# Row maxima of attention scores read two PSUM banks at a time, with thirteen of the first group's units inside the first stage's last step

## The reference

```python
x = L0_attn_query                                      # 8 x 1024 x 256, float32
x = x + 0.5 * _L0_ffn_ref(_layernorm(x), ...)          # two matrices, top-2 gate over 7 logits
x = x + _L0_attn_ref(_layernorm(x), ...)               # 16 heads of 16 columns, causal
x = x + 0.5 * _L0_ffn_ref(_layernorm(x), ...)

# _L0_attn_ref, b = 8, t = 1024, D = 16
q = q / math.sqrt(D)
scores = jnp.einsum('bhqd,bhkd->bhqk', q, k)
scores = jnp.where(causal[None, None], scores, -inf)
attn = jax.nn.softmax(scores, axis=-1)
out = jnp.einsum('bhqk,bhkd->bhqd', attn, v)
```

## Time and profile before

| | us |
|---|---|
| median of 3 runs | 1353.83 (1350.99 to 1354.71) |
| the profiled execution | 1353.6 |
| its span, first to last instruction | 1351.8 |
| PE, DVE, ACT, POOL busy | 1245.0, 1138.3, 920.7, 435.0 |
| mean granted clock of PE | 0.963 |

### The profile page before, as it was taken

How to read it: one execution, slowest core, us unless ns; L and a number is a source line. 1 busy time by engine, 2 the same in 40 slices (tenths; PEclk the granted TensorE clock), 3 DMA queues, 4 the chain that set the end, 5 groups by cost and what they waited for, 6 DMA issues and landing times. The chain is left out here.

```text
span 1351.8 us, 37753 instructions
## 1 busy us (share of the span) xinstructions
PE 1245.0 (92%) x9324; PEld 825.8 (61%) x9324; DVE 1138.3 (84%) x4510; ACT 920.7 (68%) x1858; POOL 435.0 (32%) x843
## 2 busy tenths in 40 slices
PE   4999999978999999999999999999999997699996
PEld 3988888964554454554554554554554543599996
DVE  4788888749999999999999999999999994367775
ACT  3666666630777777777777777777777777356654
POOL 3333333301222222222222222222322322467772
PEclk9999999985899999999999999999999999699998
DMA  3366666881564564664664664664664663556651
GB/s 113 141 225 225 225 225 225 220 274 37 78 107 81 99 106 80 101 104 80 103 102 80 103 102 80 104 101 80 106 99 80 106 99 107 158 180 196 192 165 63
DMA packets 121900, 174.12 MB, mean 129 GB/s; under 512 B 44012, under 2 KB 71788, under 8 KB 121804
## 3 DMA queue, kind: packets, MB, share of 16 engines
q1 hardware_dynamic: 121816, 173.30, 56.4%
HBM read 96.08 MB, written 76.02 MB: 127 GB/s over the span
## 5 line engine op out<-in xcount | busy, mean ns | idle before, releaser
L1000 ACT ACTIVATE b_probs<-bank 128x512 f32<-128x512 f32 x1152 | 597.4, 612 | 135.4 <-PE bank L1124 131.6
L1027 DVE CUSTOM_DVE_ANT_0 b_junk<-bank,mask 128x512 bf16<-128x512 f32 (+3 forms) x1032 | 446.8, 488 | 1.4 <-issue 1.2
L1030 DVE TENSOR_REDUCE b_pm<-bank 128x1 f32<-128x512 f32 x516 | 322.4, 683 | 19.7 <-PE bank L1101 18.7
L1143 PE MATMUL bank<-b_probs,b_vx 128*32 128x512 f32 (+3 forms) x3072 | 310.3, 499 | 4.2 <-ACT b_o L985 1.9
L1124 PE MATMUL bank<-qs,ks 50*128 50x512 f32 (+3 forms) x1056 | 293.6, 383 | 4.3 <-ACT b_probs L1000 0.4
L1101 PE MATMUL bank<-ks,qs 48*128 48x512 f32 (+3 forms) x1056 | 277.2, 390 | 10.9 <-PEq L443 6.3
L1101 PEld LDWEIGHTS bank<-ks,qs 48*128 48x128 f32 x1056 | 165.1, 193 | 134.6 <-DVE b_pm L1030 61.5
L145 POOL TENSOR_TENSOR hold_pool<-zero 128x1 f32<-128x1 f32 x192 | 37.4, 195 | 629.9 <-ACT b_probs L1000 474.3
L1124 PEld LDWEIGHTS bank<-qs,ks 50*128 50x128 f32 x1056 | 159.7, 188 | 57.3 <-ACT b_probs L1000 52.4
L960 POOL TENSOR_SCALAR_AFFINE_SELECT b_probs<-b_probs 128x512 f32<-128x512 f32 x256 | 158.5, 638 | 0.0
L1143 PEld LDWEIGHTS bank<-b_probs,b_vx 128*32 128x32 f32 x3072 | 71.1, 109 | 109.6 <-issue 80.9
(11 more groups left out here) (120 smaller groups left out, 1993.8 us busy)
## 6 DMA issues: line engine op xcount, KB each, us to landing
scr_qk<-a_qk SPq DMA_DIRECT2D x64, 512.0 KB, 3.2
qs<-scr_qk SPq DMA_DIRECT2D x132, 128.0 KB, 4.5
ks<-scr_qk SPq DMA_DIRECT2D x132, 128.0 KB, 5.1
scr_o<-b_o SPq DMA_DIRECT2D x64, 256.0 KB, 3.7
b_qs<-scr_qk SPq DMA_DIRECT2D x66, 128.0 KB, 4.0
b_ks<-scr_qk SPq DMA_DIRECT2D x66, 128.0 KB, 4.6
a_x<-x SPq DMA_DIRECT2D x16, 512.0 KB, 3.5
scr_x<-a_x SPq DMA_DIRECT2D x16, 512.0 KB, 2.7
```

Of the source, the lines that this page charges most:

```text
L1000: act.activation(probs[:, PROB_BUF[s], h, :], score_bank(g, t, last)[:], ACT.Exp).then_inc(p_ready, 1)
L1027: ins = dve.tensor_tensor_reduce(junk[:, t % MB, off:off + w], src, mask[:, BANK - w:BANK], 1.0, 0.0, ALU.add, ALU.max, pm[:, g.buf, 0, pl ...
L1030: ins = dve.tensor_reduce(pm[:, g.buf, 1, place(h), i:i + 1], src, AX.X, ALU.max)
L1143: last = pe.matmul(o_bank[2 * D * h:2 * D * (h + 1), col:col + w], vx[g.buf][:, j, h, :], probs[:, PROB_BUF[src], h, off:off + w], start=( ...
```

## The change

A maximum unit is now two banks wide: 1024 columns, filled by PE in two tiles and read by DVE with one instruction for each block of 128 queries in it, across the border of the banks (`dve_unit`). All are of the masked kind. A group has 18 units in place of 36 tiles; the plain maxima and the joining of halves fall away, and `part` has two steps. A unit's two tiles are of the same half of the partitions. The four banks are now two pairs, and PE fills a pair when DVE has read all of it. PE's order in a slot becomes maximum, score, three times, then the values, maximum, score, and the maxima stand one tile further ahead. Thirteen of the first group's 18 units move into stage A: into its last step and among the last chunk's projections, whose banks are chosen anew (`last_bank`).

```diff
+UNITS = ([unit_of((5, h), (1, h)) for h in range(GH)] + [unit_of((4, h), (2, h)) for h in range(GH)] +
+         [unit_of((6, h), (0, h)) for h in range(GH)] + [unit_of((3, s), (3, s + 2)) for s in range(2)] +
+         [unit_of((7, h)) for h in range(GH)])
+UNITS = UNITS[:12] + UNITS[14:] + UNITS[12:14]
+UNITS_IN_A = 13
...
+    def pe_unit_tile(self, pe, qs, ks, u, half, bank):
+
+        for i, h, k0, w, off in UNITS[u][0][half]:
+            last = pe.matmul(bank[:, off:off + w], qs[head_rows(h, SROWS), h // 2, i * P:(i + 1) * P],
+                             ks[head_rows(h, SROWS), h // 2, k0:k0 + w], start=True, stop=True)
+        last.then_inc(self.m_tile, 1)
+
+    def dve_unit(self, dve, buf, u, pair):
+
+        for i, h, off, w in UNITS[u][1]:
+            ins = dve.tensor_tensor_reduce(self.junk[:, u % 2, off:off + w], pair[:, off:off + w], self.mask[:, 2 * BANK - w:2 * BANK],
+                                           1.0, 0.0, ALU.add, ALU.max, self.pm[:, buf, head_place(h), i:i + 1])
+        ins.then_inc(self.m_read, 1)
...
             ln2.dve_low(dve, NCHUNK - 1)
-            for i in range(NQK):
-                low(NCHUNK - 1, i)
+            maximum(3)
+            for i, units in enumerate(((4,), (5, 6, 7), (8,), range(9, UNITS_IN_A))):
+                low(NCHUNK - 1, i, last=True)
+                for u in units:
+                    maximum(u)
...
+            max_unit(3)
+            for j in range(QKV):
+                qkv(NCHUNK - 1, (j,), last=True)
+                max_unit(4 + j)
+            for u in range(4 + QKV, UNITS_IN_A):
+                max_unit(u)
...
+            def max_tile(g, t):
+                u = t // 2
                 if t == 0:
                     pe.wait_ge(stacked[g.buf], g.turn(STACK, STACK))
-                if not (g.first and t < MB):
-                    pe.wait_ge(m_read, g.at(TILES, t - MB + 1))
...
+                if t % 2 == 0 and not (g.first and u < 2):
+                    pe.wait_ge(m_read, g.at(NUNIT, u - 1))
+                ahead.pe_unit_tile(pe, qs[g.buf], ks[g.buf], u, t % 2, m_bank[t % MB])
...
                 for s in range(NSLOT):
-                    score_tile(g, s, 0, last)
-                    maxima(s, 0)
...
+                    for n in range(GH):
+                        maxima(s, n)
+                        score_tile(g, s, n, last)
+                        if n == GH - 2:
+                            event(g, s)
+                            if s == TURN_SLOT and not last:
+                                turn_m(g.next(1))
```

More of the change, by code:

```diff
@@ L53 @@
 PAIRS = GH // 2
[L56 removed]
+S_ORDER = (1, 0, 2, 3)
 NBUF = 3
@@ L86, with unit_of, head_place, head_rows @@
 PROB_BUF[LOW_DONE] = 3
-MAX_SLOTS = [
[9 rows of a table removed]
-]
-EARLY = (B - 1) * H
+def unit_of(*tiles):
+    pieces, reads, at = [[], []], [], 0
+    for i, h in tiles:
+        reads.append((i, h, at, (i + 1) * P))
+        for k0 in range(0, (i + 1) * P, BANK):
+            w = min(BANK, (i + 1) * P - k0)
+            pieces[at // BANK].append((i, h, k0, w, at % BANK))
+            at += w
+    assert at == 2 * BANK and all(sum(p[3] for p in bank) == BANK for bank in pieces)
+    return pieces, reads
+UNITS = ([unit_of((5, h), (1, h)) for h in range(GH)] + [unit_of((4, h), (2, h)) for h in range(GH)] +
+         [unit_of((6, h), (0, h)) for h in range(GH)] + [unit_of((3, s), (3, s + 2)) for s in range(2)] +
+         [unit_of((7, h)) for h in range(GH)])
+UNITS = UNITS[:12] + UNITS[14:] + UNITS[12:14]
+NUNIT = len(UNITS)
+assert NUNIT % 2 == 0 and all(t[1] % 2 == u % 2 for u in range(NUNIT) for t in UNITS[u][1])
+EARLY = (B - 1) * H
+UNITS_IN_A = 13
+def head_place(h):
+    return h % 2 * PAIRS + h // 2
+def head_rows(h, n):
+    return slice(h % 2 * HALF, h % 2 * HALF + n)
 SB, MB = 3, 4
+UNITS_AHEAD = AHEAD * GH // 2
 TURN_SLOT = NSLOT - AHEAD
@@ L575, in _, with high @@
             ln1.act_high(act, 0)
-            def high(c, j, first):
+            def high(c, j, first, last=False):
                 kind, i = PROJ[j]
@@ L669, in step @@
                 ffn.dve_gate(dve, c)
+                if not nxt:
+                    maximum(0)
                 if prev:
@@ L1052, in next_maxima @@
             def next_maxima(g):
-                for a in range(AHEAD):
-                    for h in range(GH):
-                        if a == 0 and h < 3:
-                            part(g, h)
-                        maximum(g.next(1), a, h)
+                for u in range(UNITS_AHEAD):
+                    if u < 2:
+                        part(g, u)
+                    maximum(g.next(1), u)
             def step(g, last):
@@ L1601, in macaron @@
         ar = Arena(nc, ctx)
-        psum = [ctx.enter_context(nc.psum_tensor(f"bank{n}", [P, BANK], F32)) for n in range(8)]
+        pairs_of_banks = [ctx.enter_context(nc.psum_tensor(f"banks{n}", [P, 2 * BANK], F32)) for n in range(4)]
+        psum = [pairs_of_banks[n // 2][:, n % 2 * BANK:(n % 2 + 1) * BANK] for n in range(8)]
         ident = ar.sb("ident", [P, P])
```

172 lines of the change are left out of this document (85 added, 87 removed), and 9 rows, old and new, of the table MAX_SLOTS.

## The result

The changed kernel takes 1320.91 us (median of 4 runs, 1318.77 to 1322.49) where the kernel before, run beside it, takes 1352.41 (4 runs, 1349.7 to 1354.71): a ratio of 0.9767, 95% interval 0.9742 to 0.9792. It is 2.3% faster. The forecast was 1326.5, with a range from 1312 to 1345. The profiled execution took 1320.54, its span is 1318.7, 33.1 less than the span before.

A forecast was written before the change was run, and what follows sets the result against it. A loop of PE and ACT, 2.64 us a slot, was taken to bound the kernel, DVE beside it. From 1353.6 us, -13.0 (opening and stage A's end) and -14.1 (30 groups) gave 1326.5, range 1312 to 1345.

The forecast's parts named there:

- The transpose of slot 6: Transpose of the maxima, once a group: its wait for DVE's second split should go, 0.72 us a group, at most 0.80.
- a + 2.5 for the split, a + 2.64 for PE: From a, the maximum tile's start behind slot 5's values: second split at a + 2.5, PE at the transpose at a + 2.64.
- The coarser ring: Steady slots: a unit's first tile waits until two whole banks are read; costs 0.25 us a group, bounds nothing to 1.2.
- a slot of 2.8 or more makes me wrong on the ring: Test set for ordinary slots: values should stand 2.64 to 2.75 us apart; 2.8 or more would refute the ring's cost.
- DVE's unit: DVE's reading of a two-bank unit: bounds about 1.1 and 1.24 us, 1.24 taken; alone it gives nothing.
- The opening: Start of attention: five units at 1.3 us, 6.5 where 22.97 stood, 16.5 less; one more tile before the first score, 0.5.
- Stage A's end: Thirteen units moved into the first stage make it end 3.0 us later, at 309.3; bounds 1 and 6.
- The first group: First group of attention, partly at the lower clock: loses in filling units what it wins at its transpose; put at nothing.
- The rule on the same half: PE's maximum tile behind score 0 in one half of the partitions: by the rule a weight load shows; sum has nothing.
- The rival: Same half: a weight load shows at each of nine meetings, at most 0.1 us each, 0.9 a group, 1353; chance 0.03.

The follow-up runs named there:

- b_parts: The kernel before with the three steps that make the negative maxima back to back, ahead of the next group's first tile; 1330.28 us, ratio 0.9838.
- a_dve: The changed kernel with one more DVE instruction behind each unit, setting 64 columns to zero; 1328.35 us, ratio 0.9833.
- a_eight: The changed kernel with eight units in the first stage in place of thirteen, units 4 to 7 behind the last projections; 1322.37 us, ratio 0.9784.
- a_again: The changed kernel itself measured once more, beside the kernel before; 1320.41 us, ratio 0.9781.
- a_none: The changed kernel with no unit in the first stage, all 18 of the first group at the opening of attention; 1329.65 us, ratio 0.9858.
- a_four: The changed kernel with only units 0 to 3 in the first stage, ahead of the last chunk's projections; 1328.66 us, ratio 0.9841.
- b_split: The kernel before with b_parts' edit and the product with the values of six slots in two halves, as in a_split; 1408.64 us, ratio 1.0401.
- a_split_dve: a_split with a small DVE instruction (64 columns set to zero) behind each unit, as in a_dve; 1324.62 us, ratio 0.9806.
- a_noshift: The changed kernel with the maxima one tile less ahead and the order of the score tiles changed with it; 1752.19 us, ratio 1.2954.
- a_split: The changed kernel with the product with the values of six slots in two halves, the first behind score 0; 1310.63 us, ratio 0.9705.
- a_split4: As a_split, but only four products halved (slots 7, 8, 0 and 1), those of slots 3 and 6 whole; 1318.94 us, ratio 0.9752.

## Why the prediction was right, and where it was off

The sign, the mechanism and the range held. By its terms, against the 27.1 us forecast and the 33.1 measured in the profiled executions:

- **The transpose of slot 6**: forecast 0.72 a group, at most 0.80. Measured 0.80: the whole lateness went, and not only the part that the trace books as a wait. b_parts shows the cause by itself. The reasoning by instants (a + 2.5 for the split, a + 2.64 for PE) held.
- **The coarser ring**: forecast 0.25 a group within 0 to 1.2. Measured 0.13. It lies in two slots (2.68 and 2.73 for 2.64), and not as 0.05 in each of six. I had said that a slot of 2.8 or more makes me wrong on the ring; nine of the 30 groups have one, those in which the program's loop turns, and in the other 21 the same slot takes 2.74 at most. So by its own mark the forecast fails in every third group, and the mark was badly set: it caught the turn of the loop, for which the forecast had no term, with the ring. a_dve confirms that little slack is left.
- **DVE's unit**: at most 1.24 was forecast for most; 1.23 and 1.15 are measured. Reading across the border of two banks costs nothing seen.
- **The opening**: forecast -16.5; from attention's first load to the first transpose it was 26.1 before (306.27 to 332.35) and is 9.5 now (312.73 to 322.2), 16.6 less. From there to the first score I added 0.5, and it is 1.4 (4.45 before, 5.85 now): the tiles that now stand ahead of the score are the first of units, which wait for DVE at the low clock.
- **Stage A's end**: forecast +3.0, within 1 to 6. Measured +6.5 (306.27 to 312.73), outside the bounds. The last projections began at 290.05, as I had said (290.2). The step that failed is the next: "I find about 303.8 now" for the last correction, which doesn't follow from its own terms. PE is busy without a break there: 11.4 us of projections and five units between them make 290.2 + 11.4 + 5 times 0.5 to 0.9, 304 to 306 for PE's end alone, and the correction comes 0.7 behind. It stands at 306.89. The projections took 11.7 and the five units 1.26, 1.14, 0.72, 0.71 and 0.66, 4.5 together: the first two, at a clock of 0.50, cost more than the 0.9 allowed for. a_eight shows the same from the other side: with nothing between the projections the correction is back at 300.68. A unit between the last projections is not hidden by DVE's idle time, because PE is what the stage's end waits for.
- **The first group** was put at nothing. From the first score on, 33.1 - 8.75 = 24.4 are left: 20.1 in the 30 groups from 348.70 on (30 times 25.28 - 24.61), 3.6 behind the last transpose, 0.6 in the first group.
- **The tail**: 3.6 us less behind the last transpose, of which the sum has nothing. No edit lies there. In the profiled executions of a_again, a_none, b_parts, a_dve, a_four and a_eight this stretch takes 230 to 234 us, and 234 to 237 in the four with halved products, so most of it is the scatter of an execution and no gain.

Sum: -8.75 at the first score where -13.0 was forecast, -20.1 in thirty groups where -14.1 was, and -4.2 in the rest where none was. The forecast lay 5.6 us above the median because two errors, of 4 and 6 us, mostly cancelled and the tail came on top.

**The rule on the same half.** Two pieces of a tile in the same half start 0.12 apart (715.47 and 715.59), and the nine meetings of a maximum tile with a score of its own half cost, with everything else of the ring, 0.13 a group. The rival priced each of them at up to 0.1.
The Trainium skill ("TensorE: Matmul & The Clock Gate", Part 3) lets a weight load overlap only with matmuls of another row group. The loads of both pieces start at 715.48, where the first piece has just started (715.47), and the second piece follows at 715.59; so for these the trace doesn't agree with the rule.

```profile
715.48 0.19 PEld L428 LDWEIGHTS banks<-b_ks,b_qs 48*128 48x128 f32 x2
```

## What to carry to other kernels

Find the loop that sets the pace slot by slot, and then the one place in a period where something else is late: here three small DVE instructions in the wrong order were worth nine tenths of the steady gain of a far larger rewrite. Work moved into an earlier stage was free here beside the stores and two thirds free ahead of the last projections; put among matmuls that the stage's end waits for, it is moved and not hidden. When a loop is opened, add up each engine's own work in a slot for the next bound, above all that of the engine in the loop.

## What the runs showed of the hardware that I had not expected

TensorE's clock can fall to its lower level, 1.2 GHz (0.50), in the midst of steady work. In b_split it did so once in every group, at the long product of slot 5, after stretches in which PE was busy for 1.80 and 1.93 of 2 us; in a_split_dve it did so in four groups, again at that product. In a_noshift, where PE waited a fifth of the time, the mean of long stretches was 0.67 to 0.81. The two kernels with halved products on units of two banks and nothing else (a_split, a_split4) kept 1.00 through the steady groups. What in the work decides this is left open: I can name the place and the price (2.79 us for 1.50), not the cause. It means that an edit worth a tenth of a us in a slot can come with a loss of 2.7 us a group (27.31 in b_split's steady groups, 24.66 in b_parts').
